# Three waits for landed gathers in each sub-block, on the queue that gathers

## The reference

```
samp = bilinear_sample(img, iy, ix, Hin, Win)      # 4 corners each
samp = samp.reshape(N, GROUP, H, W, P, Cg)         # P = 9 taps, Cg = 32
y = einsum('nghwpc,nhwgp->nhwgc', samp, mask_sm)   # weighted by the mask
x = x + gamma1 * layer_norm(y @ w_out + b_out, ...)
m = gelu(x @ w_fc1 + b_fc1) @ w_fc2 + b_fc2
x = x + gamma2 * layer_norm(m, ...)
```

## Time and profile before

| | us |
|---|---|
| median of 3 runs | 8978.42 |
| lowest, highest | 8974.17, 8980.24 |
| profiled execution, from first to last instruction (span) | 14670.7 |
| PE busy in the profiled execution | 7831.1 |
| ACT busy | 6815.4 |
| DVE busy | 6704.9 |
| POOL busy | 6413.8 |

### The profile page before, as it was taken

One profiled execution on the slowest core, in us unless ns is written; L12 is line 12 of the kernel. 1 busy time (PEld: TensorE's weight loads), 2 busy tenths in 40 slices (PEclk: granted clock), 3 DMA queues, 4 the chain that ended last, 5 costly groups with the idle time before them and its releaser, 6 DMA issues.

```text
span 14670.7 us, 162317 instructions
## 1 busy us (share of the span) xinstructions
PE 7831.1 (53%) x48435; PEld 3785.6 (26%) x48435; DVE 6704.9 (46%) x19495; ACT 6815.4 (46%) x8248; POOL 6413.8 (44%) x6711
## 2 busy tenths in 40 slices
PE   4445655455555555555554555555555455444567
PEld 2122222222222222222222222222222222222234
DVE  4444434444444444444444444454444444344333
ACT  0234634455444554445444454444544355443465
POOL 4544444444444444444444444444444444444430
PEclk6667767777777777777777777777777777776778
DMA  2111111111111111111111111111111111222325
GB/s 64 41 50 39 36 38 39 46 41 38 37 41 49 36 40 38 42 49 34 40 37 46 45 34 39 38 48 44 37 39 35 51 40 37 55 62 63 107 58 162
DMA packets 559311, 703.51 MB, mean 48 GB/s; under 512 B 256976, under 2 KB 371536, under 8 KB 556288
## 3 DMA queue, kind: packets, MB, share of 16 engines
q0 software_dynamic: 214624, 439.98, 11.0%
q1 hardware_dynamic: 343808, 252.97, 6.1%
HBM read 579.54 MB, written 112.84 MB: 47 GB/s over the span
## 4 chain that ended last, share of the span: by engine, by line
another core or an unknown queue 37%; ACT 17%; DVE 16%; issue 13%; PE 12%; DVEq 5%; DMA 1%; SPq 0%; ACTq 0%
ACT tanh L1882 14%; PE score_ps L2072 5%; DVEq L1347 5%; DVE pool_mem L1564 2%; PE side_ps L2012 1%; DVE y L1573 1%; PE value_ps L2101 1%; PE side_ps L1982 1%; DVE expoT L1641 1%; ACT L1892 1%; DVE pool_mem L1551 1%; PE turn_ps L1951 1%; ACT L1867 1%; ACT expo L1892 1%
## 5 line engine op out<-in xcount | busy, mean ns | idle before, releaser
L1882 ACT ACTIVATE tanh<-key_rep,query 128x896 f32<-128x896 f32 (+7 forms) x6400 | 5565.3, 951 | 4618.0 <-remote 2987.3
L1328 POOL DMA_INDIRECT pool_mem<-patches_odd,pool_mem x3375 | 3226.1, 956 | 4002.7 <-DVE y L1573 2977.5
L1328 POOL DMA_INDIRECT pool_mem<-patches_even,pool_mem x3332 | 3187.6, 957 | 3857.4 <-DVE y L1573 2815.5
L2072 PE MATMUL score_ps<-tanh,score_w 128*32 128x512 f32 (+3 forms) x24320 | 3461.1, 604 | 1933.9 <-ACT tanh L1882 1057.1
L2072 PEld LDWEIGHTS score_ps<-tanh,score_w 128*32 128x32 f32 x24320 | 826.2, 120 | 3979.9 <-issue 2624.8
L2101 PE MATMUL value_ps<-values,expoT 128*128 128x129 f32 (+1 forms) x5200 | 908.4, 317 | 408.3 <-issue 329.7
L1564 DVE TENSOR_TENSOR pool_mem<-pool_mem 128x384 f32<-128x384 f32 (+1 forms) x2352 | 1089.1, 532 | 12.9 <-issue 7.6
L1573 DVE TENSOR_REDUCE y<-pool_mem 128x64 f32<-128x2304 f32 x392 | 999.1, 2549 | 31.9 <-issue 9.6
L2012 PE MATMUL side_ps<-near_map,hatT 112*64 112x480 f32 x2792 | 806.3, 685 | 318.6 <-DVEq L1347 206.0
L2101 PEld LDWEIGHTS value_ps<-values,expoT 128*128 128x128 f32 (+1 forms) x5200 | 790.6, 223 | 524.8 <-issue 399.8
L1892 ACT ACTIVATE expo<-score_ps,tiny 128x896 f32<-128x896 f32 (+9 forms) x416 | 383.4, 922 | 1017.1 <-remote 743.1
(11 more groups left out here) (194 smaller groups left out, 8060.3 us busy)
## 6 DMA issues: line engine op xcount, KB each, us to landing
pool_mem<-in_weight SPq DMA_DIRECT2D x64, 1024.0 KB, 9.3
pool_mem<-patches_odd,pool_mem POOLq DMA_INDIRECT x3375
pool_mem<-patches_even,pool_mem POOLq DMA_INDIRECT x3332
patches_even<-pool_mem SPq DMA_DIRECT2D x104, 256.0 KB, 2.0
patches_odd<-pool_mem SPq DMA_DIRECT2D x104, 256.0 KB
pool_mem<-in_x SPq DMA_DIRECT2D x56, 224.0 KB
x_tok<-in_x SPq DMA_DIRECT2D x192, 64.0 KB
x_d<-x SPq DMA_DIRECT2D x192, 64.0 KB
```

What stands on the lines that cost most here:

```text
L1328: pool.indirect_dma_start(gathered[:, b, j * 4 * CG:(j + 1) * 4 * CG], None, patches_flat[int(odd)], bass.IndirectOffsetOnAxis(ap=index[:, ...
L1882: nc.scalar.activation(tanh[:, TANH_AT[ui][0]:TANH_AT[ui][1]], key_rep[:, lo:lo + w], ACT.Tanh, bias=query[:, col:col + 1]).then_inc(tanh_ ...
L2072: last = mm(score_ps[32 * col:32 * col + 32, ci % 2, lo:hi], score_w[:, place], tanh[:, TANH_AT[ui][0] + lo:TANH_AT[ui][0] + hi], start=pl ...
```

## The change

At the 5th, 9th and 13th gather of each sub-block (j = 4, 8, 12), GpSimd first waits until all gathers issued so far into the current slot have landed, those of earlier sub-blocks and images included, and increments `pool_step` once more. Nothing else is changed, neither the order on the other engines nor the planner's constants.

```diff
@@ -41,6 +41,7 @@
 GATHERED = SAMPLES - 1
 NEAR = SAMPLES - 1
 FULL_FROM = 0
+PAUSES = (4, 8, 12)
 SPANS, SPAN = 4, 14
@@ -1323,7 +1324,11 @@
 
                     pool.wait_ge(sampled.sem, sampled.after(n, last_user(t)))
                     nc.gpsimd.sem_inc(pool_step, 1)
+                    landed = n * (SLOT_USES[b] * 16 * GATHERED) + 16 * sum(columns(n, u) for u in range(t) if gather_slot(u) == b)
                     for j in range(columns(n, t)):
+                        if j in PAUSES:
+                            pool.wait_ge(gather_done[b], landed + 16 * j)
+                            nc.gpsimd.sem_inc(pool_step, 1)
                         at = tt * SAMPLES + j
                         pool.indirect_dma_start(
                             gathered[:, b, j * 4 * CG:(j + 1) * 4 * CG], None, patches_flat[int(odd)],
```

## The result

The changed kernel takes 11468.49 us (median of 4 runs, 11460.77 to 11482.85), the kernel before 8979.26 us on the same occasions: ratio 1.2775, 95% interval 1.276 to 1.279, or 2489 us more. The direction and the mechanism were forecast; 11,100 us was too low, and 11,468 us lies above the range's end of 11,400.

A forecast was written before the change was run, and what follows sets the result against it. GpSimd's unbroken gathers were taken to bound the kernel; 1176 pauses of 2.3 + 0.78 - 1.25 = 1.83 us add 2152 us: 8978 + 2152 - 30 = 11,100 us, range 10,650 to 11,400 us for 8 in 10.

The forecast's parts named there:

- The direction and the mechanism: Whole kernel: slower, 96%; GpSimd pays each pause in full, 76%, giving 11,100 us.
- What bounds the kernel: Unprofiled kernel: GpSimd gathers without a break and sets the pace, with 6 to 124 us of waiting in all.
- the sum of GpSimd's parts: GpSimd's head, gathers with their gaps, and tail: 73 + 8502 + 397 = 8972 us, against 8978 us measured.
- The pauses and their count: Before gathers 4, 8 and 12 of each sub-block: 1176 pauses, each lasting until the newest gather has landed.
- The restart: GpSimd's queue after a satisfied wait: 0.78 us until the next gather starts.
- The rival of a cheap restart: After a short wait the next gather is already prepared: 1.08 us a pause, 10,220 us in all; chance 8%.
- The landing: From a gather's start to the arrival of its semaphore: 2.3 us, with ends 1.95 and 2.5 us.
- The packets' end: Last packets of a gather, read from 0.1 us slices: up to 1.95 us after its start, the landing's lower bound.
- The row of `w_key`: SP's direct load late in a burst, landing in 3.3 us; kept for the rival of dearer pauses, chance 10%.
- What is absorbed: GpSimd's present waiting of 6 to 124 us, which pauses would cover; 30 us taken off.
- the step that would have passed anyway: Plain pace from one gather's start to the next, 1.25 us, subtracted from each pause's cost.
- The wait that I gave for a pause in the profile: New row of 1176 GpSimd waits for its own DMAs, each about 0.3 (gap) + 1.5 us.

The follow-up runs named there:

- The second recording: The kernel before, unchanged, recorded once more on another occasion: span 8975.4 us, with GpSimd waiting 1.2 us in all for DVE.
- the row of one, three and six pauses: Changed kernel with one, three or six pauses for each sub-block: 9815.78, 11468.49 and 13961.11 us; 2.09, 2.12 and 2.11 us a pause.
- the run with 16 gathers: Kernel before with 16 gathers in place of 17 in sub-blocks that have 17, 17th sample left out: 8620.35 against 8977.46 us, ratio 0.9597.

## Why the prediction was right and where it was wrong

- **What bounds the kernel** was right, and it was the step on which all hung: the page of the earlier trace rows showed an engine that waits 40% of the span, and the sum of GpSimd's parts showed that it can't. The second recording, the row of one, three and six pauses and the run with 16 gathers confirm it. That the sum came within 6 us of the time was luck: the stretched recording gave a gather's pace 0.006 us too short (1.268 for 1.274 us, about 40 us in all) and a tail 38 us too long (397 for 359 us), and the two cancel; the product given as 8502 us is 8504 us besides.
- **The pauses and their count** were right: 1176, all real.
- **The restart**, 0.78 us from the semaphore to the next gather, was right: 0.02 + 0.02 + 0.73 in the chain above, 0.78 us in the mean of all pauses. The rival of a cheap restart falls. The pause isn't from start to landing alone: this restart, which a full queue hides, is a third of its price.
- **The landing was the term of the sum that was mis-sized.** I took 2.3 us from a gather's start to its semaphore, with 1.95 and 2.5 as ends; it measured 2.66 us in the mean. Two steps made it too small.
  - The packets' end was misread. The slices of the earlier trace rows put a packet with its whole duration where it starts, not where it ends. In the same trace of before, the last packet of the gather at 7015.69 ends 2.14 us after the gather's start, not at 1.9 us; in the trace of the change the last one ends at 2.19 us in the median, 0.24 us over the 1.95. The 0.35 us that I added for the semaphore were right: from 2.19 to 2.53 us are 0.34.
  - A usual value was used where the sum needs a mean: the median is 2.53 us, and late landings add 0.13 us.

  So 0.24 + 0.13, less 0.01, are the 0.36 us that were missing. My upper end of 2.5 us lay under the median, and this is why the range ended too low. The row of `w_key`, 3.3 us in the earlier trace rows, I had set aside for a rival; such landings are part of the usual mix. Of the pauses in which packets of SP's queue start between the gather's first packet and the release (about 200 of 1176) the mean step is 3.77 us, without them 3.37 us; that goes with traffic, but no run took the traffic away.
- **What is absorbed**: nothing by waiting, as there were 1.2 us of it. But a little came from elsewhere. Between the second recording of before and that after: 1176 steps by 3.438 - 1.278 = +2540 us, the other 5530 steps of 1.268 in place of 1.273 us = -31, the tail 345 in place of 359 us = -14, together 2495, measured 8975.4 to 11471.6 = 2496.
- In numbers of the forecast: 2.3 to 2.66 us is +0.36 on 1176 pauses, +423 us; the restart of 0.776 in place of 0.78 us takes back 5 us, and the step that would have passed anyway, 1.278 in place of 1.25 us, 33 us; 44 us absorbed in place of 30, -14. 11,100 + 371 = 11,471, near the 11,468 us measured.
- **In the profile after** I forecast that the waits for DVE would shrink because the pauses cover them, and that the span would grow little or not at all. The span fell, but not for that reason: the standstills of the earlier trace rows just didn't occur again. That this part came out was luck. The wait that I gave for a pause in the profile, 0.3 + 1.5 us, also doesn't fit my own step of 3.1 us, which leaves 2.1 us beside a gather of 0.96; it measured 2.47 us.

The rule of the Trainium skill (DMA: Bandwidth & Descriptors, Anatomy of one DMA, SWDGE path), 2.0 us and the bytes at 436 GB/s, gives an estimate of 2.15 us for 64 KB. It fits the end of the last packet (2.19 us in the median) and not the semaphore (2.53 us in the median, 2.66 in the mean); the time that followed from it, 10,920 us, was 550 us too low. The measurement decides.

## What to carry to other kernels

Before costing a change, sum up each engine's own instructions at their steady pace, with head and tail, and hold the sum against the unrecorded time: here an engine with 44% busy in the profile was the one that set it. Such a sum can meet the time by errors that cancel, so it needs a recording whose span is the program's own time. On a queue that sets the pace, a wait for its own newest transfer cost the whole landing and the restart behind it, less one step; leaving two newer ones in flight brought it from 2.12 to 0.09 us. Where a term is paid 1176 times, take its mean with the late ones, and read a landing where a semaphore ends a wait, not from the slices of a view of packets.

## What the runs showed that I had not expected

One recorded execution can be 63% longer than the same program's next recording (14670.7 and 8975.4 us), with the single durations on GpSimd, DVE and ACT as usual, PE's longer at a lower granted clock, and 5793 us of waits of GpSimd for DVE that the next recording doesn't have (1.2 us). A met wait between two gathers is free to within 0.1% of the time even 1176 times (ratio 1.0000, 0.9991 to 1.0009). And a gather's landing hardly depends on its bytes here: 0.22 us for 48 KB, at the same number of packets. Most of it lies before the first packet, 1.65 us.
